# Four chained attention blocks on one core: splitting q and k straight out of the bank, VectorE masks on scores instead of probabilities, and a new step order

## The chip, the cores and the metric

One core of a Trainium2 chip runs the whole program in one launch. The metric is the device time of that core in microseconds (us), lower is better. Of the engines, PE (TensorE) multiplies and writes into eight accumulator banks of 128 partitions by 512 float32 ("bank"), ACT (ScalarE) and DVE (VectorE) read the banks and work in SBUF, POOL (GpSimd) works in SBUF alone here, and SP (SyncE) issues nearly all DMAs. Each engine runs its own instructions in order and waits for the others by semaphores.

## The reference

`x` is (32, 256, 256), `ctx_1024` is (32, 120, 256), all float32. Four blocks follow one another, and each batch element is independent of the others:

```
L0: x += causal self attention(LN(x));  x += cross attention(LN(x), ctx);  x += gelu-MLP(LN(x))
L1: x = LN(x + self attention(x), masked by mask_SxS_ik1); x = LN(x + cross attention(x, ctx)); x = LN(x + relu-MLP(x))
L2: x = LN(x + cross attention(x, ctx), masked by mask_BxSxS2_bk1)     16 heads of 16
L3: x = LN(x + cross attention(x, ctx))                                16 heads of 64
attention: scores = q.k / sqrt(d); masked ones -> minus infinity; p = softmax(scores); out = p.v
```

## The kernel before

**Passes.** Three passes of 32 elements each: l0, l1 and l2 (L2 and L3 together). Between passes x goes through DRAM. In each pass the elements are software-pipelined: several stages of neighbouring elements are in flight at once, and each engine's instruction stream interleaves them.

**What sets the order.** `LISTS` holds for each pass and engine one list of steps with due times, such as `scores_exp.own.0/1.3973`: kind, stage, index, and a time counted in elements. `Step` adds START of the pass and the element's number, `run` sorts all steps of an engine by that time, and this is the order in which the engine's code is written. The banks are handed out by a walk over PE's list: each PE step takes the bank that is free first, by the due time of the step that reads it. Due times only order; they never delay. `SPREAD` stretches the times of single elements at the ends of a pass. "own" is the first attention of a pass, "other" the second, "ff" the MLP, "three" is L3 and "c" the context.

**q and k in three bf16 parts.** For exact scores q and k are split as hi + mid + lo (bf16 each), and the parts are stacked along the contraction. Before the change: PE `project_q`/`project_k` fills a bank; ACT copies it with the bias into a float32 tile (`ot_raw`, for "other" inside `other_words`) and frees the bank; DVE casts hi (L949), subtracts it (L953) and casts mid (L959); POOL subtracts mid for lo (L663). SP spills each part to DRAM as it is ready (L519) and loads the stack back (L533, into `qstack`/`kstack`). PE `scores_max` then multiplies the stacks, DVE takes row maxima (L1002 with the mask added in the bank, L1006 without), splits them too (`negate`), PE turns them (`negate_t`), DVE copies them (`nm_t`, L1048), SP puts them below the stack as extra rows (`nm_rows`, L538), and PE's `scores_exp` makes transposed scores minus the maximum. ACT takes exp (L760) into `probs`, PE's `probs_v` multiplies by v.

**Masks at scores_exp.** l0 (causal): POOL zeroes the blocked half of the probabilities (L649). l1: for each of 16 heads PE adds the mask with one more matmul, `mask_less` by `identb`, 512 columns (`exp_on` = "pe"). l2: DVE takes the minimum of the probabilities and a mask after exp (`mask_probs`, L1022, `probs_own` and `m_cols`, both in SBUF).

**Normalisation** is DVE `stats` (L891 to L899), POOL `stats` (L594, L600), DVE `norm` (L911, `xh`), then a turn on PE (L1208) that ACT copies out.

## Time and profile before

| | us |
|---|---|
| median of 3 runs | 4791.93 |
| lowest, highest | 4788.07, 4794.76 |
| the profiled execution: its time, its span | 4792.18, 4790.4 |
| PE, PE's weight loads busy | 4512.8 (94%), 3551.8 (74%) |
| DVE, ACT, POOL busy | 3884.1 (81%), 2368.0 (49%), 1381.1 (29%) |

The page is one execution. Busy time of PE has modelled ends, so two matmuls that start 0.22 us apart can show 0.38 us each; the distance of starts tells the rate. The three passes have different limits, so the tables are read for stretches inside each: l0 until about 1510 us, l1 from about 1700 to 3090, l2 from about 3240. The half-speed slices of PE's clock stand at the start, at the borders of the passes, and singly in l2.

### The profile page before, as it was taken

To read this page: it belongs to the slowest core of one execution; us is meant where nothing else is said; L and a number is where in the kernel's file an instruction comes from. 1 tells how busy PE (TensorE), PEld (TensorE's weight loads), DVE (VectorE), ACT (ScalarE), POOL (GpSimd) and SP (SyncE) were. 2 spreads that over 40 slices of the span, in tenths; PEclk is the share of its full clock that TensorE was granted. 3 is DMA by queue.
4 is the path that set the end of the run, shared out by engine and by line. 5 is a ranking of instruction groups with operands and counts; after the bars stand their busy time and mean duration, and the time that the engine had idled before them with its cause. 6 is when DMAs were issued, how large, how long until landed. Compare 5 with 4: busy or idle time off the path is not lost. (4 is left out here: it accounts for less than half of the span.)

```text
span 4790.4 us, 97864 instructions
## 1 busy us (share of the span) xinstructions
PE 4512.8 (94%) x34560; PEld 3551.8 (74%) x34624; DVE 3884.1 (81%) x11141; ACT 2368.0 (49%) x6433; POOL 1381.1 (29%) x1813
## 2 busy tenths in 40 slices
PE   5999999999998899999999999979999999999998
PEld 4777777777777677777777777767777777777776
DVE  4888888888888788888888888857787787878786
ACT  2555555555454444444434343435555555555555
POOL 3333333333333133333323232321212121211212
PEclk8999999999999999999999999989999999999999
DMA  5444444444444444444444444321222212121221
GB/s 156 133 138 128 135 126 140 120 147 119 146 120 141 124 121 139 121 136 131 141 127 131 129 125 134 114 83 57 72 57 62 66 57 71 52 77 52 68 61 32
DMA packets 393272, 513.31 MB, mean 107 GB/s; under 512 B 109136, under 2 KB 360784, under 8 KB 371280
## 3 DMA queue, kind: packets, MB, share of 16 engines
q1 hardware_dynamic: 385392, 496.82, 35.5%
q10 hardware_dynamic: 7392, 10.24, 0.7%
q8 instruction: 276, 4.52, 0.4%
q14 instruction: 212, 1.74, 0.1%
HBM read 266.30 MB, written 236.72 MB: 105 GB/s over the span
## 5 line engine op out<-in xcount | busy, mean ns | idle before, releaser
L760 ACT ACTIVATE probs_own<-bank 128x384 f32<-128x384 f32 (+2 forms) x1280 | 598.2, 582 | 282.7 <-remote 156.5
L594 POOL TENSOR_SCALAR veps<-meanvar 128x2 f32<-128x2 f32 x256 | 63.1, 247 | 1503.3 <-DVE meanvar L899 1501.8
L1146 PE MATMUL bank<-ht,w_ff 128*128 128x256 f32 x2048 | 490.9, 383 | 0.8 <-issue 0.8
L1146 PE MATMUL bank<-w_ff,ffh 128*128 128x256 f32 x2048 | 491.1, 383 | 0.0
L1146 PE MATMUL bank<-qstack_own,kstack_own 99*128 99x256 bf16 (+2 forms) x2560 | 395.1, 265 | 31.9 <-DMA qstack_own<-nm_t_own 26.3
L1146 PEld LDWEIGHTS bank<-w_ff,ffh 128*128 128x128 f32 x2048 | 377.8, 192 | 46.8
L1146 PEld LDWEIGHTS bank<-ht,w_ff 128*128 128x128 f32 x2048 | 376.8, 191 | 46.9 <-issue 1.9
L1002 DVE CUSTOM_DVE_ANT_0 bank<-bank,mask_rows 128x256 f32<-128x256 f32 x1024 | 393.1, 474 | 2.9 <-PE bank L1146 2.9
L680 ACT ACTIVATE ht<-bank,columns_l 128x256 f32<-128x256 f32 x384 | 198.7, 578 | 382.8 <-PE bank L1208 382.6
L825 ACT ACTIVATE probs_other<-bank,negmax 128x120 f32<-128x120 f32 x1024 | 354.7, 382 | 64.4 <-DVE negmax L1126 64.2
L1146 PE MATMUL bank<-kstack_own,qstack_own 96*128 96x256 bf16 (+2 forms) x3072 | 355.4, 245 | 28.2 <-DMA qstack_own<-q_parts 19.9
L1146 PE MATMUL bank<-probs_own,v_aug_own 128*32 128x256 f32 (+2 forms) x5120 | 310.7, 368 | 53.7 <-DVE probs_own L1022 51.7
L1146 PEld LDWEIGHTS bank<-kstack_own,qstack_own 96*128 96x128 bf16 x3072 | 255.1, 98 | 107.7 <-issue 24.7
L1006 DVE TENSOR_REDUCE nmf_other<-bank 128x4 f32<-128x480 f32 x512 | 306.4, 644 | 33.8 <-PE bank L1146 33.4
L1146 PEld LDWEIGHTS bank<-qstack_own,kstack_own 99*128 99x128 bf16 (+1 forms) x2560 | 224.8, 105 | 142.9 <-DMA qstack_own<-nm_t_own 45.7
L1146 PE MATMUL bank<-ht,w_own 128*128 128x256 f32 x1280 | 314.4, 390 | 3.3 <-ACT ht L680 2.6
L760 ACT ACTIVATE probs_other<-bank 120x512 f32<-120x512 f32 x512 | 275.6, 607 | 76.0 <-PE bank L1146 75.9
L1002 DVE DVE_READ_ACCUMULATOR2_ANT nmf_own<- 128x1 f32 x2048 | 312.1, 152 | 0.0
L635 POOL TENSOR_TENSOR xb<-xh,vectors_l 128x512 f32<-128x512 f32 x160 | 213.5, 1334 | 289.6 <-issue 286.4
L663 POOL TENSOR_TENSOR other_parts<-other_words,other_parts 128x240 bf16<-128x240 f32 (+1 forms) x128 | 122.8, 970 | 580.1 <-issue 329.5
L1146 PEld LDWEIGHTS bank<-probs_own,v_aug_own 128*32 128x32 f32 (+1 forms) x5120 | 133.8, 109 | 187.8 <-DVE probs_own L1022 99.8
L1146 PEld LDWEIGHTS bank<-ht,w_own 128*128 128x128 f32 x1280 | 235.9, 192 | 46.5 <-issue 13.7
(166 smaller groups left out, 10673.6 us busy)
## 6 DMA issues: line engine op xcount, KB each, us to landing
qstack_own<-q_parts SPq DMA_DIRECT2D x96, 768.0 KB, 6.2
...
other_words<-k_parts SPq DMA_DIRECT2D x64, 360.0 KB, 3.7
```

The lines of the kernel that those rows point to most:

```text
L594: nc.gpsimd.tensor_scalar(veps[key][:, :], meanvar[key][:, :, 1], r["norms"][key]["eps"], None, ALU.add).then_inc(veps_ready.sem, 1)
L635: nc.gpsimd.tensor_tensor(xb[key][:, :, :], xh[src][:, :, :], mul[:, None, :].broadcast_to((P, QT, C)), ALU.mult).then_inc(xb_half.sem, 1)
L663: nc.gpsimd.tensor_tensor(f3[2], x32, f3[1], ALU.subtract).then_inc(lo_ready.sem, 1)
L680: return nc.scalar.activation(out, in_, ACT.Identity, scale=scale, bias=bias)
L760: nc.scalar.activation(probs[key][0:rows, j % a.slots, 0:n], bank_of(u)[0:rows, 0:n], ACT.Exp, scale=a.scale).then_inc(a_done.sem, 1)
L825: ins = nc.scalar.activation(probs3[:, j % 4, n, :], bank[:, n * S2:(n + 1) * S2], ACT.Exp, scale=-1.0, bias=negmax3[:, j, n:n + 1], accum ...
L1002: ins = v.tensor_tensor_reduce(scores, scores, add, -1.0, LIMIT if a.masked == "each" else 3.0e38, ALU.add, ALU.min, nmf[key][:, t, at:at ...
L1006: ins = v.tensor_reduce(nmf[key][:, t, first:first + FT * len(heads) - FT + 1:FT], bank[:, 0:len(heads) * nk].rearrange("p (h k) -> p h k" ...
L1146: return nc.tensor.matmul(out, lhsT, rhs, start=first, stop=True, skip_group_check=True)
```

## The change

1. **Split out of the bank.** ACT's copy to float32 goes. ACT writes hi (bf16) straight from the bank with the bias (`split_hi`). DVE computes (bank + bias) - hi into the float32 tile (`split_rest`; with a bias two SCALAR_TENSOR_TENSORs, one per half) and this frees the bank. ACT casts mid from that tile (`split_mid`). POOL's lo stays. Both DVE casts go.
2. **Masks of VectorE on scores.** `mask_probs` on DVE becomes `mask_scores`: DVE adds the mask (0 or -2^100) in the bank before exp, and exp waits for it. l2 does this for all 8 steps of an element. l1 goes from "pe" to "half": of 16 heads the 8 odd ones keep PE's mask matmul, the 8 even ones are masked by DVE. l0's POOL mask stays.
3. **l2's v copies.** `project_v` (now `project_v2`) and `project_v3` are copied out by ACT instead of DVE.
4. **New tables.** All of LISTS, START (l1 31.9 to 32.1, l2 64.4657 to 64.6), SPREAD emptied. Unused set-up of the old mask goes (`mask_cols`, a once-only PE step).

In the diff, `split_hi`, `split_mid` and the wait ahead of exp are ACT's code, the copy with `x32` as output and the addition of the mask are DVE's.

```diff
-START = {"l0": 0.0, "l1": 31.9, "l2": 64.4657}
+START = {"l0": 0.0, "l1": 32.1, "l2": 64.6}
-    "l0": {-2: (0.0, 0.9969)},
+    "l0": {},
...
-            turn.0.0/0.3084 project_q.own.0/0.6711 project_k.own.0/0.7099 scores_exp.own.0/1.4122 scores_exp.own.7/1.4222
+            turn.0.0/0.1721 split_hi_q.own.0/0.4346 split_hi_k.own.0/0.5024 split_mid_q.own.0/0.5224 split_mid_k.own.0/0.5687
...
+LAST_BY_DVE = {"project_q": "split_rest_q", "project_k": "split_rest_k"}
...
+            elif kind in ("split_hi_q", "split_hi_k"):
+                src = bank_of(u, ("project_" + x, key, 0))[:, 0:FT * nt].rearrange("p (f t) -> p f t", f=FT)
+                hi = parts[:, 0, :].rearrange("p (f t) -> p f t", f=FT)
...
+                if bias is None:
+                    copy(hi, src).then_inc(hi_ready.sem, 1)
+                else:
+                    nc.scalar.activation(hi[:, 0, :], src[:, 0, :], ACT.Identity, bias=bias[:, 0:1])
+                    nc.scalar.activation(hi[:, 1, :], src[:, 1, :], ACT.Identity, bias=bias[:, 1:2]).then_inc(hi_ready.sem, 1)
+            elif kind in ("split_mid_q", "split_mid_k"):
...
+                copy(parts[:, 1, :].rearrange("p (f t) -> p f t", f=FT), x32).then_inc(mid_ready.sem, 1)
...
+                if w.new(masked_by_dve, ("mask_scores", key, j)):
+                    act_e.wait_ge(masked_by_dve.sem, w.value(masked_by_dve, ("mask_scores", key, j)))
...
+                if bias is None:
+                    ins = v.tensor_tensor(x32, src, hi, ALU.subtract)
                 else:
+                    for f in range(FT):
+                        ins = v.scalar_tensor_tensor(x32[:, f, :], src[:, f, :], bias[:, f:f + 1], hi[:, f, :], ALU.add, ALU.subtract)
...
-                v.tensor_tensor(p, p, most, ALU.min).then_inc(masked_by_dve.sem, 1)
+                v.tensor_tensor(p, p, add, ALU.add).then_inc(masked_by_dve.sem, 1)
...
-              "dve", "pe")
+              "dve", "half")
```

What the tables move, at three places. First PE in l1, at the start of a burst of `scores_exp` of "own" (banks with their numbers; `d_done`, `a_done` are DVE's and ACT's counts). Before:

```order
L1146 MATMUL bank0<-qstack_own,kstack_own 128x256 [waits d_done]
L1146 MATMUL bank0<-qstack_own,kstack_own 128x256
L1146 MATMUL bank0<-mask_less,identb 128x512
L1146 MATMUL bank1<-qstack_own,kstack_own 128x256 [waits d_done]
L1146 MATMUL bank1<-qstack_own,kstack_own 128x256
L1146 MATMUL bank1<-mask_less,identb 128x512
L1146 MATMUL bank4<-qstack_own,kstack_own 128x256 [waits d_done]
L1146 MATMUL bank4<-qstack_own,kstack_own 128x256
L1146 MATMUL bank4<-mask_less,identb 128x512
```

After:

```order
L1156 MATMUL bank0<-qstack_own,kstack_own 128x256 [waits d_done]
L1156 MATMUL bank0<-qstack_own,kstack_own 128x256
L1156 MATMUL bank0<-mask_less,identb 128x512
L1156 MATMUL bank5<-qstack_own,kstack_own 128x256 [waits a_done]
L1156 MATMUL bank5<-qstack_own,kstack_own 128x256
L1156 MATMUL bank5<-mask_less,identb 128x512
...
L1156 MATMUL bank1<-qstack_own,kstack_own 128x256 [waits d_done]
L1156 MATMUL bank1<-qstack_own,kstack_own 128x256
L1156 MATMUL bank0<-qstack_own,kstack_own 128x256 [waits a_done]
L1156 MATMUL bank0<-qstack_own,kstack_own 128x256
L1156 MATMUL bank5<-qstack_own,kstack_own 128x256 [waits a_done]
L1156 MATMUL bank5<-qstack_own,kstack_own 128x256
```

Every head had its `mask_less` matmul; now only the odd ones have one, and the heads stand in an order that mixes both kinds, in more banks.

Second DVE in l1, around the splits of "own". Before (the splits of "own", `q_parts_own` and `k_parts_own`):

```order
L949 CAST q_parts_own<-ot_raw_own 128x512 [waits a_done,spilled_q_own]
L953 TENSOR_TENSOR ot_raw_own<-ot_raw_own,q_parts_own 128x512 [waits hi_ready]
L959 CAST q_parts_own<-ot_raw_own 128x512 [waits rest_ready,spilled_q_own]
L949 CAST k_parts_own<-ot_raw_own 128x512 [waits a_done,spilled_k_own]
L953 TENSOR_TENSOR ot_raw_own<-ot_raw_own,k_parts_own 128x512 [waits hi_ready]
L959 CAST k_parts_own<-ot_raw_own 128x512 [waits rest_ready,spilled_k_own]
L1107 TENSOR_TENSOR xn_own<-bank5,xb_0 128x512 [waits xhat_ready,xb_ready,d_full]
```

After (eight mask additions per element, `bank` and `mask_less`, stand among the other work; two stretches of it):

```order
L1032 TENSOR_TENSOR bank3<-bank3,mask_less 128x512 [waits a_full]
L1032 TENSOR_TENSOR bank1<-bank1,mask_less 128x512 [waits a_full]
L1032 TENSOR_TENSOR bank0<-bank0,mask_less 128x512 [waits a_full]
...
L1085 TENSOR_TENSOR ctx_q_own<-ot_raw_own,rec_own 128x2x8x16 [waits recip_ready]
L1085 TENSOR_TENSOR ctx_q_own<-ot_raw_own,rec_own 128x2x8x16
L984 SCALAR_TENSOR_TENSOR ot_raw_own<-bank1,columns_l1,q_parts_own 128x256 [waits divided,hi_ready]
L984 SCALAR_TENSOR_TENSOR ot_raw_own<-bank1,columns_l1,q_parts_own 128x256
L943 TENSOR_SCALAR xh_2<-xn_other,meanvar_2,rstd_2 128x256 [waits xb_half,rstd_ready,moments_ready]
L943 TENSOR_SCALAR xh_2<-xn_other,meanvar_2,rstd_2 128x256
L984 SCALAR_TENSOR_TENSOR ot_raw_own<-bank6,columns_l1,k_parts_own 128x256 [waits hi_ready]
L984 SCALAR_TENSOR_TENSOR ot_raw_own<-bank6,columns_l1,k_parts_own 128x256
```

Six instructions of the two splits have become four, each with a bank among its inputs, and `xh_2` stands between them.

Third POOL in l0, from the causal masks (L649) to the sums of the next stage. Before:

```order
L663 TENSOR_TENSOR k_parts_own<-ot_raw_own,k_parts_own 128x512 [waits spilled_k_own,mid_ready]
L594 TENSOR_SCALAR veps_1<-meanvar_1 128x2 [waits moments_ready]
L600 TENSOR_TENSOR rstd_1<-veps_1,half 128x2 [waits veps_ready,xhat_ready]
L663 TENSOR_TENSOR q_parts_own<-ot_raw_own,q_parts_own 128x512 [waits spilled_q_own,mid_ready]
L629 TENSOR_TENSOR xb_0<-x_in,vectors 128x512 [waits d_done,x_loaded]
L663 TENSOR_TENSOR other_parts<-other_words,other_parts 128x240 [waits spilled_k_other,mid_ready]
```

After:

```order
L664 TENSOR_TENSOR k_parts_own<-ot_raw_own,k_parts_own 128x512 [waits spilled_k_own,mid_ready]
L664 TENSOR_TENSOR q_parts_own<-ot_raw_own,q_parts_own 128x512 [waits spilled_q_own,mid_ready]
L634 TENSOR_TENSOR xb_0<-x_in,vectors 128x512 [waits d_done,x_loaded]
L599 TENSOR_SCALAR veps_1<-meanvar_1 128x2 [waits moments_ready]
L605 TENSOR_TENSOR rstd_1<-veps_1,half 128x2 [waits veps_ready,xhat_ready]
L634 TENSOR_TENSOR xb_1<-xn_own,vectors 128x512 [waits d_done]
```

`stats_1` (`veps_1`, `rstd_1`, which DVE's `xh_1` waits for) stood between the two lo parts, with `q_parts_own` and `xb_0` right behind it; now both lo parts and `xb_0` stand ahead of it.

## Rows read from the trace of the kernel before

**Rows 1.** The page, part 1: busy us (share of the span) x instructions.
```profile
PE 4512.8 (94%) x34560; PEld 3551.8 (74%) x34624; DVE 3884.1 (81%) x11141; ACT 2368.0 (49%) x6433; POOL 1381.1 (29%) x1813
```

**Rows 2.** Windows of 500 us in l0, l1, l2: length, busy of each engine, PEclk, DMA share, GB/s.
```profile
1000.00:1500.00 500.00, 470.75 (x3803) 382.72 (x3792) 424.13 (x910) 262.69 (x621) 180.36 (x299) 1.00 0.45 134
2000.00:2500.00 500.00, 498.35 (x3750) 390.23 (x3769) 435.18 (x1347) 218.57 (x475) 164.41 (x173) 1.00 0.46 136
...
3500.00:4000.00 500.00, 478.70 (x3592) 369.28 (x3591) 400.25 (x1343) 283.75 (x995) 100.03 (x104) 0.99 0.22 63
```

**Rows 3.** Tile nm_t_own on DVE, per pass: ns min/median/max, first and last start.
```profile
L1048 DVE COPY nm_t_own<-bank x30: 282/283/284, 136.1 to 1508.8; 48x256 bf16<-48x256 bf16 x30
...
L1048 DVE COPY nm_t_own<-bank x28: 273/274/282, 1732.1 to 3040.9; 48x256 bf16<-48x256 bf16 x28
...
L1048 DVE COPY nm_t_own<-bank x29: 281/283/284, 3339.8 to 4713.8; 48x256 bf16<-48x256 bf16 x29
```

**Rows 4.** Waits of PE, 1000 to 1500: us in total, times, longest.
```profile
PE bank L1208 <- DVE xh L911: 15.8, 11, 1.8
PE bank L1298 <- DVE nm_parts_own L1041: 7.5, 10, 0.9
PE bank L1146 <- DMA qstack_own<-nm_t_own: 5.7, 10, 0.7
```

**Rows 5.** Waits of PE, 2000 to 3000: the longest.
```profile
PE bank L1146 <- DMA qstack_other<-nm_t_other: 0.7, 3, 0.3
```

**Rows 6.** Waits of PE, 3500 to 4500: the longest.
```profile
PE bank L1146 <- DVE probs_own L1022: 33.4, 40, 1.1
```

**Rows 7.** Timeline of PE in l1: start us, us, instruction.
```profile
2414.68 0.38 PE L1146 MATMUL bank<-qstack_own,kstack_own 99*128 99x256 bf16 x2
2414.90 0.38 PE L1146 MATMUL bank<-mask_less,identb 128*128 128x512 bf16 x1
2415.12 0.38 PE L1146 MATMUL bank<-qstack_own,kstack_own 99*128 99x256 bf16 x2
```

**Rows 8.** Groups of DVE by form, 2000 to 3000: busy us, mean ns.
```profile
L953 DVE TENSOR_TENSOR ot_raw_own<-ot_raw_own,k_parts_own 128x512 f32<-128x512 f32 x20 | 30.5, 1526 | 0.7
...
L953 DVE TENSOR_TENSOR ot_raw_own<-ot_raw_own,q_parts_own 128x512 f32<-128x512 f32 x20 | 13.9, 693 | 0.7
...
L949 DVE CAST q_parts_own<-ot_raw_own 128x512 bf16<-128x512 f32 x20 | 8.5, 427 | 2.3
...
L959 DVE CAST other_parts<-other_words 128x240 bf16<-128x240 f32 x21 | 5.8, 278 | 0.0
```

**Rows 9.** Timeline of DVE in l1: reads of a bank, back to back.
```profile
2413.10 0.68 DVE L1107 TENSOR_TENSOR xn_ff<-bank,xb 128x512 f32<-128x512 f32 x1
2413.71 0.42 DVE L974 TENSOR_TENSOR other_words<-bank,vectors_l 120x256 f32<-120x256 f32 x1
2414.05 0.42 DVE L891 BATCH_NORM_STATS2 moments<-xn_ff 128x6 f32<-128x256 f32 x1
```

**Rows 10.** Timelines of DVE and POOL in l0, the same microseconds.
```profile
822.03 2.44 DVE L911 TENSOR_SCALAR xh<-xn_own,meanvar,rstd 128x256 f32<-128x256 f32 x2 [0.68 <-POOL rstd L600]
...
821.88 1.16 POOL L663 TENSOR_TENSOR q_parts_own<-ot_raw_own,q_parts_own 128x512 bf16<-128x512 f32 x1
823.00 1.31 POOL L629 TENSOR_TENSOR xb<-x_in,vectors 128x512 f32<-128x512 f32 x1
```

**Rows 11.** Lines L1022 and L1107 in l2, 3300 to 4700.
```profile
L1022 DVE TENSOR_TENSOR probs_own<-probs_own,m_cols x228: 677/680/1811, 3299.9 to 4675.6; 120x512 f32<-120x512 f32 x114
...
L1107 DVE TENSOR_TENSOR xn_own<-bank,x_in x29: 691/692/693, 3307.9 to 4681.8; 128x512 f32<-128x512 f32 x29
```

**Rows 12.** Timeline of DVE in l2: one element's masks.
```profile
3933.35 7.08 DVE L1022 TENSOR_TENSOR probs_own<-probs_own,m_cols 120x512 f32<-120x512 f32 x8 [0.72 <-ACT probs_own L760]
```

**Rows 13.** Groups of ACT, 500 to 1500: SBUF to SBUF.
```profile
L788 ACT ACTIVATE ff_xu<-ff_xu 128x512 f32<-128x512 f32 x84 | 53.5, 636 | 66.8 <-DVE ff_xu L1113 65.8 <-issue 1.0
```

**Rows 14.** Stack of k in l2: timeline of SP, median us to landing, timeline of PE.
```profile
3961.85 0.32 SPq L533 DMA_DIRECT2D kstack_own<-k_parts  x1
...
kstack_own<-k_parts SPq DMA_DIRECT2D x20, 360.0 KB, 6.0
...
3968.29 0.80 PE L1146 MATMUL bank<-kstack_own,qstack_own 96*128 96x120 bf16 x12
```

**Rows 15.** Timeline of PE at the border from l1 to l2.
```profile
3154.39 0.44 PE L1217 MATMUL bank<-identb,m_rows 128*120 128x128 bf16 x2 [10.02 <-DVE m_rows L925]
```

More of the change, by code:

```diff
@@ L46 @@
 PASSES = ("l0", "l1", "l2")
-START = {"l0": 0.0, "l1": 31.9, "l2": 64.4657}
+START = {"l0": 0.0, "l1": 32.1, "l2": 64.6}
+STAGE = {"own": 0, "0": 0, "x": 0, "c": 0, "m": 0, "other": 1, "1": 1, "ff": 2, "2": 2, "three": 2, "3": 2}
 SPREAD = {
-    "l0": {-2: (0.0, 0.9969)},
+    "l0": {},
     "l1": {},
@@ L120 @@
+            store.x.0/4.1837 loads.first.0/0.03 loads.rest.0/4.00 loads.rest.1/4.25 loads.rest.2/4.50 loads.rest.3/4.75
             loads.rest.4/5.00 loads.rest.5/5.25 loads.rest.6/5.50 loads.rest.7/5.75 loads.rest.8/6.00 loads.rest.9/6.25
@@ new lines @@
+            scores_max.own.0/1.4320 scores_max.own.1/1.4369 scores_max.own.5/1.4805 scores_max.own.4/1.4853
+            scores_max.own.7/1.4902 scores_max.own.3/1.5338 scores_max.own.6/1.5386 project_k3.three.0/1.5920
+            negate_t.own.0/1.6343 mask.m.0/1.6757 project_v2.own.0/1.6783 scores_exp.own.6/1.7102 scores_exp.own.4/1.7151
+            scores_exp.own.1/1.7201 scores_exp.own.3/1.7250 scores_exp.own.5/1.7397 scores_exp.own.7/1.7446
+            project_k3.three.1/1.7496 scores_exp.own.0/1.7897 scores_exp.own.2/1.7946 probs_v.own.2/1.8226 probs_v.own.3/1.8323
@@ L240 @@
+            nm_rows.own.0/1.6525 store.x.0/3.7906
         """,
@@ L357, in run @@
     when = {e: {(u.tag, u.element): u.at for u in steps} for e, steps in plan.items()}
-    masked = {(u.tag, u.element) for e in ("DVE", "POOL") for u in plan[e] if u.tag[0] == "mask_probs"}
+    masked = {(u.tag, u.element) for u in plan["POOL"] if u.tag[0] == "mask_probs"}
     banks = [ctx.enter_context(nc.psum_tensor(f"bank{i}", [P, 512], F32)) for i in range(8)]
@@ L366, in run @@
         _, b = min(free)
-        by = "ACT" if kind in READ_BY_ACT else "DVE"
-        read = (kind, key, j // 2) if kind == "probs_v" else u.tag
+        by = "ACT" if kind in READ_BY_ACT and kind not in LAST_BY_DVE else "DVE"
+        read = (kind, key, j // 2) if kind == "probs_v" else (LAST_BY_DVE[kind], key, 0) if kind in LAST_BY_DVE else u.tag
         holds[u.tag, u.element] = b, holder.get(b)
@@ L840, in _ @@
                      bank_of(u)[0:S2, :].rearrange("p (t f x) -> p t f x", t=QT, f=2)).then_inc(a_done.sem, 1)
+            elif kind == "project_v3":
+                if w.new(a_full, u.tag):
+                    act_e.wait_ge(a_full.sem, w.value(a_full, u.tag))
+                if first and j == r["first_of"]["project_v3"]:
+                    for x in "qk":
+                        reuse(act_e, w, u, spilled[x, "other"], [("spill_" + x, "other", i) for i in range(PARTS)], u.element - 1)
+                for tag in w.latest_first(a_full, [("probs_v3", "three", i) for i in range(2 * j, 2 * j + 2)], 1):
+                    if w.new(a_full, tag, 1):
+                        if w.twice:
+                            settle(act_e)
+                        act_e.wait_ge(a_full.sem, w.value(a_full, tag, 1))
+                copy(v3[:, 512 * j:512 * j + 512], bank_of(u)[0:S2, :]).then_inc(a_done.sem, 1)
             elif kind == "probs_v3":
@@ L1180, in _ @@
                 pe.wait_ge(setup_g, SETUP_ALL)
-            if kind == "masks":
-                pe.wait_ge(setup_v, len(make_masks[0]))
-                bank = take(u)
-                for t in range(QT):
-                    ins = nc.tensor.matmul(bank[:, t * P:(t + 1) * P], none_rows[:, t, :], ident[:, :], start=True, stop=True,
-                                           skip_group_check=True)
-                ins.then_inc(d_full.sem, 1)
-            elif kind == "context":
+            if kind == "context":
                 if w.new(c_loaded, ("load_c", "c", 0)):
```

480 lines of the change are left out of this document (222 added, 258 removed).

## The prediction

> **What bounds the kernel now.** I read the page first: PE is busy 94% of the span, DVE 81%, ACT 49% [rows 1]. An average over three passes says little, so next the windows, one inside each pass: PE is busy 470.75 of 500 us in l0, 498.35 in l1 and 478.70 in l2, DVE 424, 435 and 400 [rows 2]. l1 has no idle PE to give back, l0 and l2 have. The tile `nm_t_own` is written once per element, so its first and last start give the period of each pass [rows 3]: l0 (1508.8 - 136.1) / 29 = 47.33 us, l1 (3040.9 - 1732.1) / 27 = 48.47 us, l2 (4713.8 - 3339.8) / 28 = 49.07 us. Whatever the change does comes 31 times per pass through these three numbers; the rest is borders.
>
> Then PE's waits, divided by the elements in the window. In l0 500 / 47.33 = 10.6 elements: 15.8 us for `xh`, 7.5 us for `nm_parts_own` and 5.7 us for the DMA of the negated maxima [rows 4], which is 1.50, 0.71 and 0.54 us per element, 2.75 together. In l1 the longest wait is 0.7 us in 1000 [rows 5]: PE's own work is the limit. In l2 (1000 / 49.07 = 20.4 elements) the wait for DVE's masked probabilities is 33.4 us [rows 6], 1.64 us per element.
>
> **l1: eight mask matmuls less.** A `mask_less` matmul starts at 2414.90 and the next scores at 2415.12 [rows 7]: it takes 0.22 us of PE's pace (the 0.38 us shown is its modelled end). Eight go per element: 8 x 0.22 = 1.76 us. PE's floor becomes 48.47 - 1.76 = 46.7 us.
>
> DVE takes what PE gives, and it is the fuller of the others: 435.18 / 500 x 48.47 = 42.2 us per element [rows 2]. What changes there:
> - Added: eight additions over 512 columns of a bank. The trace has no plain addition that writes a bank, but a TENSOR_TENSOR reading a bank at 2413.10 lets the next one start at 2413.71 [rows 9], 0.61 us. Bounds for one: 0.6 us from that row, and above 1.53 us, the slowest row of a 512 column operation [rows 8]. I take 0.61, since operation, shape and source are the same: +4.9 us.
> - Removed: eight casts per element, six over 512 columns at up to 0.43 us and two over 240 at 0.28 [rows 8]: -3.1 us.
> - Changed: the subtraction, now out of the bank in two halves. Halves of 256 columns out of a bank are 0.34 us apart [rows 9], so 0.68 for two against 0.69 for the old one [rows 8], equal. But `k_parts_own`'s old subtraction took 1.53 us in the mean for the same work [rows 8]; if that goes, -0.8 us.
>
> Sum: +1.0 to +1.8 us, so DVE has 43.2 to 44.0 us of work in a period of at least 46.7. It still fits, with 2.7 to 3.5 us to spare instead of 6.3. With less room some handoffs will show on PE; l0 and l2 show 2.75 and 2.0 us of idle PE at more room than that, though from single slow operations. I charge 0.5 us (bounds 0 and 1.76, where nothing is left of the gain): l1 gains 1.25 us per element.
>
> **l2: the mask ahead of exp.** Masks of one element take 7.08 us for eight [rows 12], and PE's `probs_v` waits for them. The operation's median is 0.68 us and its maximum 1.81 [rows 11]: it is the same work each time, stretched by something. An addition of the same size with one operand in a bank shows 691 to 693 ns over 29 elements [rows 11], never stretched. In l0 the trace shows such a stretch beside POOL's work [rows 10], so I put this one down to POOL too. The Trainium skill, page "SBUF — State Buffer", section "Who interferes with whom", says that DVE and GpSimd share a pair of SBUF ports as an exclusive lock, and the section before it that a DVE operation takes the lock with two SBUF inputs or in a two-port mode; the trace agrees (1811 against 693 ns). By that rule the mask in the bank costs 8 x 0.61 = 4.9 us; without it, if POOL slowed this one too, still 7.08. I take the row that never stretches. The chain from the first mask to the last is then 2.2 us shorter, more than the 1.64 us that PE waits. What is late next is exp, which now runs behind the mask: one 0.6 us ACT operation after the last mask instead of one mask after the last exp, so the end comes no later. I count 1.3 of the 1.64 us. ACT takes three more bank copies per element (0.6 us each or less) at 283.75 / 500 busy [rows 2]: hidden by ACT's idle time, and it is behind nothing that PE waits for except in its own queue. Bounds 0 and 1.64.
>
> **l0: nothing leaves PE, two stalls may.** PE's 1.50 us are for `xh` of "own": its two halves take 2.44 us at 822.03 while POOL runs lo of q from 821.88 and the sum `xb` from 823.00 [rows 10]. In the new POOL order both stand ahead of `stats_1`, so at `xh_1` POOL has nothing queued but the next stage's sum. That stall should go, and `nm_parts_own`'s 0.71 likewise, if POOL's `xb` no longer meets it. The DMA's 0.54 stays. That would be 2.2 us; but `stats_1` now stands behind lo of q, which hangs on ACT and DVE, and a stall removed lets the next one through. I take 1.5 us, bounds 0 and 2.75. The dropped casts and the moved `split_mid` change no length on PE; DVE loses 3.1 us here and gains nothing, which is only room.
>
> **The split's chain.** Before: ACT copy, DVE hi, DVE rest, DVE mid, POOL lo. After: ACT hi, DVE rest, ACT mid, POOL lo. One DVE step of 0.43 us [rows 8] is gone from the chain, mid costs ACT about 0.64 us (an SBUF to SBUF operation of 512 columns [rows 13]) instead of 0.43, so it is 0.2 us shorter, plus one more crossing between engines. The hi part is ready one step earlier. ACT's work: four mids of 0.64 us or less, four hi in place of four copies. It matters, since the lead is small: in l2 SP issues the load of k's stack at 3961.85, it lands 6.0 us later at 3967.85, and PE uses it at 3968.29 [rows 14]. Every cast mid waits in ACT's queue behind exps. I count 0 (bounds -0.2 and +2 us per element). The bank of a projection is held longer, until `split_rest`; the new order has room for it, as it mixes banks more. SP issues the same loads and spills in a slightly other order.
>
> A page speaks against splitting out of the bank. The Trainium skill, page "VectorE: DVE Perf Modes", section on the TRN2 errata, gives a higher fixed cost for a PSUM source than for an SBUF one (120 against 58 cycles) and per instruction, so two halves would cost 0.78 us against 0.59 for one whole. By it DVE has 0.7 us per element more in l1 and still fits. The trace does not show this price: halves from a bank are 0.34 us apart [rows 9].
>
> **Borders.** At 3154.39 PE waits 10.02 us for the mask rows of the first element of l2 [rows 15]; the new PE list has that `mask` step half an element later, so it should go. Against it stands that all splits of a border have new neighbours, and the first stages of l1 start 0.2 elements later by START. I count 0, bounds -15 and +15 us.
>
> **Sum.** 31 x (1.5 + 1.25 + 1.3) = 31 x 4.05 = 126 us. Profiled span 4790.4, with 1.8 us around it 4792.2, which is the median of the runs (4791.93). 4792 - 126 = 4666 us.
>
> **Rivals.**
> 1. *DVE becomes the bound of l1.* For: slack falls from 6.3 to about 3 us, mask additions sit between PE and exp, and exp runs in its own order, so one late mask holds all exps behind it. Against: 43 to 44 us of work in 46.7. Then l1 gains nothing, and l0 and l2 get what is above: 31 x 2.8 = 87, or with half of that lost too 60: 4705 to 4732, say 4720.
> 2. *The stalls of l0 and l2 only move.* For: both are ends of long chains, where another link may be next. Against: both are traced to one stretched operation. Then only l1's gain stays: 31 x 1.25 = 39, at most 55: 4745.
> 3. *All idle PE goes.* l0 2.75, l1 1.76, l2 2.0: 31 x 6.5 = 202: 4590. For: less contention in every pass. Against: the DMA wait of l0 is untouched.
> 4. *Slower: mid is stuck in ACT's queue.* Place: `split_mid` of q or k, behind a row of 8 or more exps of 0.5 us, then lo, spill and stack load late, with PE's `scores_max` waiting. The lead of 0.44 us in l2 [rows 14] covers nothing. It outweighs the gain when the stack is over 126 / 93 = 1.4 us late per element. At 3 us late in all passes: 93 x 3 - 126 = +153: 4945; in one pass alone, 31 x 3 more and its own gain lost, 4790 to 4800.
> 5. *The reordering undoes it.* A step order by due times that does not fit the real durations gives new waits of about 1.3 us per element: no change, 4790.
>
> **How the numbers follow.** The forecast 0.55 (own range 4625 to 4705), rival 1 0.16, rival 2 0.12, rival 3 0.05, rival 4 0.08, rival 5 0.04. A measurement of this kernel tells about 0.2% (10 us) from no change. The range 4610 to 4755 holds the forecast, rivals 1 and 2 and half of 3. Faster 0.88, within 0.2% 0.04, slower 0.08.
>
> **What would show it.** Period of `nm_t_own`: 45.8 in l0, 47.2 in l1, 47.8 in l2. In l1 half as many `mask_less` matmuls on PE, PE still over 97% busy, DVE near 44 us of each element. In l2 the mask additions on banks at 0.68 us each with no long maximum, and `probs_v` no longer waiting for DVE for over 0.3 us. In l0 `xh_1` at 0.4 us per half. Wrong would be: mask additions over 0.8 us, PE waits in l1 over 1 us per element that end with DVE or ACT, or `scores_max` waiting for stack DMAs.

## The result, and the profile after

The changed kernel takes 4522.95 us (median of 4 runs, 4519.09 to 4525.0), the kernel before 4791.87: a ratio of 0.9438, 95% interval 0.9422 to 0.9455. That is 269 us less, where I had forecast 126 and a range that ended at 4610. The page, part 1, answers to [rows 1]:

```profile
PE 4377.2 (97%) x34368; PEld 3536.8 (78%) x34368; DVE 3512.6 (78%) x10917; ACT 2551.7 (56%) x6849; POOL 1376.6 (30%) x1813
```

The tile `nm_t_own`, one stretch inside each pass, as in [rows 3]:

```profile
L1058 DVE COPY nm_t_own<-bank x29: 275/283/283, 173.4 to 1399.1; 48x256 bf16<-48x256 bf16 x29
...
L1058 DVE COPY nm_t_own<-bank x26: 270/273/274, 1664.0 to 2838.7; 48x256 bf16<-48x256 bf16 x26
...
L1058 DVE COPY nm_t_own<-bank x30: 270/273/274, 3126.2 to 4442.9; 48x256 bf16<-48x256 bf16 x30
```

First to last start over the count less one gives the periods:

| us per element | before | forecast | after | change |
|---|---|---|---|---|
| l0 | 47.33 | 45.8 | 43.78 | -3.55 |
| l1 | 48.47 | 47.2 | 46.99 | -1.48 |
| l2 | 49.07 | 47.8 | 45.40 | -3.67 |

31 x (3.55 + 1.48 + 3.67) = 270: the periods carry the whole gain, and the borders, taken together, add nothing to it. l1 came out near the forecast. The surprise is l0 and l2.

PE's waits in l0, 500 to 1400 in both kernels, each in us, times, longest. Before, which answers to [rows 4] over more elements:

```profile
PE bank L1208 <- DVE xh L911: 27.0, 19, 1.8
PE bank L1298 <- DVE nm_parts_own L1041: 13.8, 19, 0.7
PE bank L1146 <- DMA qstack_own<-nm_t_own: 10.9, 19, 0.7
```

After, the only one:

```profile
PE bank L1156 <- DMA qstack_own<-nm_t_own: 0.2, 1, 0.2
```

All three stalls are gone, the DMA's among them. In l2 nothing waits for a masked probability any more ([rows 6] had 33.4 us).

But idle PE before was only 2.75 and 2.0 us per element. Windows inside l0 and l2 (length, PE, PEld, DVE, ACT, POOL busy, PEclk, DMA share, GB/s) show the rest. Before:

```profile
500.00:1350.00 850.00, 800.33 (x6510) 650.02 (x6509) 720.29 (x1546) 447.19 (x1059) 310.74 (x522) 1.00 0.44 131
3500.00:4400.00 900.00, 861.60 (x6470) 666.21 (x6469) 717.84 (x2410) 510.48 (x1773) 176.94 (x186) 0.99 0.22 63
```

After:

```profile
500.00:1350.00 850.00, 849.67 (x7023) 707.75 (x7022) 699.72 (x1595) 518.82 (x1229) 344.38 (x561) 1.00 0.49 144
3500.00:4400.00 900.00, 898.85 (x6992) 725.00 (x6992) 659.16 (x2488) 589.04 (x2003) 184.82 (x196) 1.00 0.23 68
```

Busy share times period: in l0 PE was busy 800.33 / 850 x 47.33 = 44.56 us per element and is now busy 43.76, for the same 362 matmuls (6510 / 850 x 47.33 and 7023 / 850 x 43.78). In l2 it was 46.98 and is 45.34. So 0.8 and 1.6 us of "busy" time did no work. A matmul is drawn 0.38 us long while the next starts 0.22 us later [rows 7]; when the next one is late, that drawn end covers the first 0.16 us of the wait. In l2 half-clock stretches add to it (PEclk 0.99). By my estimate this accounts for 3 waits x 0.16 = 0.5 of the 0.8 us in l0, and for 4 x 0.16 + 0.01 x 49 = 1.1 of the 1.6 us in l2; where the rest lies I did not find.

The other half of the story is on DVE. Groups by form (count, busy us, mean ns), l0 (500 to 1450) and l2 (3340 to 4710) before:

```profile
L911 DVE TENSOR_SCALAR xh<-xn_own,meanvar,rstd 128x256 f32<-128x256 f32 x40 | 48.7, 1257 | 14.0 <-POOL rstd L600 14.0
L1041 DVE TENSOR_TENSOR nm_parts_own<-nmf_own,nm_parts_own 128x32 bf16<-128x32 f32 x20 | 22.8, 1138 | 0.7
...
L1022 DVE TENSOR_TENSOR probs_own<-probs_own,m_cols 120x512 f32<-120x512 f32 x224 | 198.0, 952 | 20.6 <-ACT probs_own L760 20.6
L953 DVE TENSOR_TENSOR ot_raw_own<-ot_raw_own,k_parts_own 128x240 f32<-128x240 f32 x28 | 38.0, 1358 | 0.0
```

After (500 to 1390, 3130 to 4440):

```profile
L943 DVE TENSOR_SCALAR xh<-xn_own,meanvar,rstd 128x256 f32<-128x256 f32 x42 | 15.5, 411 | 30.1 <-POOL rstd L605 30.1
L1051 DVE TENSOR_TENSOR nm_parts_own<-nmf_own,nm_parts_own 128x32 bf16<-128x32 f32 x20 | 3.8, 192 | 0.7
...
L1032 DVE TENSOR_TENSOR bank<-bank,m_cols 120x512 f32<-120x512 f32 x232 | 141.7, 692 | 2.4 <-PE bank L1156 1.0
L981 DVE TENSOR_TENSOR ot_raw_own<-bank,k_parts_own 128x240 f32<-128x240 f32 x29 | 11.8, 408 | 24.4 <-ACT k_parts_own L678 24.4
```

These four were stretched before (1257, 1138, 952, 1358 ns). The first two are the same instructions and now run at their plain length (411, 192); the other two read a bank in place of SBUF and are never stretched (692, 408). One operation of l0 has taken the stretch over, where it holds up nobody: `ffh` takes 854 ns, where it took 662 in the kernel before.

```profile
L1129 DVE SCALAR_TENSOR_TENSOR ffh<-ff_xu 128x512 f32<-128x512 f32 x83 | 70.8, 854 | 0.0
```

### The profile page after: what moved, and what is told of

Read it like the earlier page. It is cut to its first block and busy times, and to the rows that moved or that the text cites. A ratio compares the mean times of both kernels' runs of the same rounds, so it can differ in the third digit from the quotient of the medians.

```text
span 4520.2 us, 97208 instructions
## 1 busy us (share of the span) xinstructions
PE 4377.2 (97%) x34368; PEld 3536.8 (78%) x34368; DVE 3512.6 (78%) x10917; ACT 2551.7 (56%) x6849; POOL 1376.6 (30%) x1813
## 5 line engine op out<-in xcount | busy, mean ns | idle before, releaser
L1156 PEld LDWEIGHTS bank<-w_ff,ffh 128*128 128x128 f32 x2048 | 379.8, 190 | 47.7 <-ACT ffh L793 0.2
L1156 PEld LDWEIGHTS bank<-ht,w_ff 128*128 128x128 f32 x2048 | 373.8, 191 | 45.7 <-issue 0.8
L1156 PE MATMUL bank<-qstack_own,kstack_own 99*128 99x256 bf16 (+2 forms) x2560 | 365.5, 263 | 16.5 <-DMA qstack_own<-nm_t_own 15.3
L640 POOL TENSOR_TENSOR xb<-xh,vectors_l 128x512 f32<-128x512 f32 x160 | 203.5, 1272 | 386.9 <-DVE xn_other L1117 311.1
L1156 PE MATMUL bank<-probs_own,v_aug_own 128*32 128x256 f32 (+2 forms) x5120 | 286.1, 362 | 8.8 <-ACT probs_own L783 5.2
L1136 DVE TENSOR_REDUCE negmax<-bank 128x4 f32<-128x480 f32 x256 | 158.2, 649 | 159.4 <-PE bank L1156 159.4
L1013 DVE CUSTOM_DVE_ANT_0 bank<-bank,m_rows 128x120 f32<-128x120 f32 x1024 | 248.7, 326 | 20.7 <-PE bank L1156 20.7
```

Of the source, the lines that this page charges most:

```text
L640: nc.gpsimd.tensor_tensor(xb[key][:, :, :], xh[src][:, :, :], mul[:, None, :].broadcast_to((P, QT, C)), ALU.mult).then_inc(xb_half.sem, 1)
L1013: ins = v.tensor_tensor_reduce(scores, scores, add, -1.0, LIMIT if a.masked == "each" else 3.0e38, ALU.add, ALU.min, nmf[key][:, t, at:at ...
L1136: v.tensor_reduce(negmax3[:, j, :], bank_of(u)[:, 0:HG * S2].rearrange("p (h k) -> p h k", k=S2), AX_X, ALU.min).then_inc(negmax3_ready.se ...
L1156: return nc.tensor.matmul(out, lhsT, rhs, start=first, stop=True, skip_group_check=True)
```

## The experiments

Fifteen kernels, each timed against the kernel before on the same chip; that one's median was between 4788.6 and 4792.1 us each time. Differences to the kernel after are between times of different rounds. The periods are means over elements 3 to 28 of l0, and over as many steady ones of l1 and l2, from the starts of `nm_t_own`.

| kernel | us | ratio to before (95%) | l0 | l1 | l2 |
|---|---|---|---|---|---|
| before | 4791 | 1 | 47.3 | 48.5 | 49.1 |
| after | 4523 | 0.9438 (0.9422 to 0.9455) | 43.8 | 47.0 | 45.4 |
| order_alone | 4937 | 1.0305 (1.029 to 1.032) | 47.1 | 51.3 | 51.4 |
| code_alone | 4868 | 1.0161 (1.0146 to 1.0176) | 47.3 | 53.3 | 47.1 |
| narrow_before | 4612 | 0.9624 (0.9608 to 0.964) | 44.9 | 48.2 | 46.4 |
| narrow_after | 4513 | 0.9419 (0.9405 to 0.9433) | 43.7 | 47.0 | 45.4 |
| order_narrow | 4717 | 0.9841 (0.9826 to 0.9856) | 44.7 | 50.5 | 47.4 |
| code_narrow | 4760 | 0.9924 (0.9904 to 0.9944) | 44.8 | 52.8 | 47.1 |
| pool_order_before | 4841 | 1.0103 (1.0086 to 1.012) | 48.9 | 48.5 | 49.0 |
| mask_bank_before | 4751 | 0.9917 (0.9902 to 0.9932) | 47.3 | 48.5 | 47.7 |
| pool_order_after | 4555 | 0.951 (0.9496 to 0.9524) | 44.8 | 47.0 | 45.3 |
| mid_on_vector | 4576 | 0.9551 (0.9535 to 0.9567) | 45.2 | 47.3 | 45.4 |
| l1_masks_pe | 4572 | 0.9544 (0.9530 to 0.9558) | 43.8 | 48.8 | 45.4 |
| project_v_early | 4579 | 0.9555 (0.9539 to 0.9571) | 45.7 | 47.0 | 45.4 |
| l1_twelve_masks | 4599 | 0.9599 (0.9584 to 0.9613) | 43.8 | 49.5 | 45.4 |
| mask_sbuf_after | 4702 | 0.9807 (0.9793 to 0.9822) | 43.8 | 47.0 | 51.3 |
| l1_tuned | 4530 | 0.9453 (0.9437 to 0.9469) | 43.7 | 47.2 | 45.4 |

### The two halves apart

In the cuts from the tables, here and below, entries of one engine stand side by side and the ones between them are left out; in the cuts of code `...` marks what is left out.

order_alone: the old code under the new tables (k of own in l0 shown):

```diff
-START = {"l0": 0.0, "l1": 31.9, "l2": 64.4657}
+START = {"l0": 0.0, "l1": 32.1, "l2": 64.6}
-ACT project_k.own.0/0.5390   DVE split_hi_k 0.5779, split_rest_k 0.5883, split_mid_k 0.6046
+ACT project_k.own.0/0.5315   DVE split_hi_k 0.5535, split_rest_k 0.5537, split_mid_k 0.5738
```

> The old code with the new tables of times: PE, ACT, POOL and SyncE in the new order; ACT still copies q and k out of the bank, DVE casts hi and mid and masks the probabilities of l2 in SBUF, PE makes all sixteen masks of l1. Two copies of l1 stand a little later than the new hi parts, since they must follow the division of the heads. Theory A (the order takes the stalls of l0 and l2 away, whatever the code): periods l0 44.2, l1 48.3, l2 46.8 us, in all 4792 - 31 x (3.1 + 0.2 + 2.3) = 4618. Theory B (the moved work does it: less on DVE, the mask in the bank, the split out of the bank; the order only adapts): the old code under the new order keeps or worsens its stalls, 4760 to 4830. Theory C (POOL no longer runs beside DVE's SBUF operations): as A in l0, where the order of POOL is the new one (44.2), but l2 keeps stretched masks and stays near 48: 4670.

Measured 4937: slower than before by 146 us, worse than any theory had. Its DVE groups in l0:

```profile
L957 DVE TENSOR_TENSOR ot_raw_own<-ot_raw_own,q_parts_own 128x512 f32<-128x512 f32 x20 | 29.7, 1486 | 0.7
L963 DVE CAST other_parts<-other_words 128x240 bf16<-128x240 f32 x20 | 27.0, 1348 | 0.0
L915 DVE TENSOR_SCALAR xh<-xn_own,meanvar,rstd 128x256 f32<-128x256 f32 x40 | 14.7, 410 | 27.7 <-POOL rstd L604 27.7
```

The new order does free `xh`. But POOL now works beside the subtraction for q and the cast of mid, and those take 1486 and 1348 ns. They are the very operations that the new code reads out of the bank or gives to ACT. l0 as a whole gains nothing (47.1). In l1, which loses 2.8 us, PE waits 21.8 us in 1000 for `ctx_t_own` and the subtraction for k is still at 1530 ns; with POOL's work cut (order_narrow, below) they are 5.1 us and 693 ns. In l2 PE waits over 3 us at a time for the masked probabilities, and then something more is lost. Timeline of PE, then windows around the wait:

```profile
3523.33 1.16 PE L1150 MATMUL bank<-vectors,probs_other 64*128 64x120 f32 x16
3527.73 3.45 PE L1150 MATMUL bank<-probs_own,v_aug_own 120*32 120x256 f32 x32 [3.24 <-DVE probs_own L1026]
3531.11 3.77 PE L1150 MATMUL bank<-w_v,ct 128*120 128x512 f32 x4
...
3538.16 1.88 PE L1150 MATMUL bank<-w_v,ct 128*120 128x512 f32 x4
```

```profile
3515.00:3527.00 12.00, 9.31 (x77) 8.11 (x75) 9.06 (x18) 6.28 (x12) 6.96 (x6) 1.00 0.08 25
3528.00:3536.00 8.00, 7.86 (x52) 2.94 (x44) 5.27 (x11) 1.48 (x8) 0.00 (x0) 0.57 0.00 0
3536.00:3550.00 14.00, 14.00 (x87) 10.76 (x84) 9.85 (x24) 10.70 (x37) 3.40 (x4) 1.00 0.29 85
```

After 3.24 us without a matmul the granted clock over 3528 to 3536 is 0.57, so most of this stretch is at the lower of its two levels (1.2 GHz), and the four matmuls of `w_v` take 3.77 us where the next four take 1.88. Over l2 the grant is 0.96 (3500 to 4400).

code_alone: the new code under the old tables; each step stands where the one that it replaces stood:

```diff
-DVE split_hi_k.own.0/0.5779 split_rest_k.own.0/0.5883 split_mid_k.own.0/0.6046
+ACT split_hi_k.own.0/0.5390 split_mid_k.own.0/0.6046   DVE split_rest_k.own.0/0.5883
```

> The new code with the old tables of times: each new step stands where the step it replaces stood (hi on ACT at the old copy, rest and mid at their old times, the masks just ahead of their exp). Theory A: the stalls of l0 stay (46.5 to 47.3), l1 gains at most its eight matmuls (47.3), l2 loses the wait for the masks alone (47.5): 4792 - 31 x (0.4 + 1.2 + 1.5) = 4696. Theory B: most of the gain is here, below 4620. Theory C: in l2 the mask in the bank no longer stretches (692 ns each instead of 952), l2 47.5; in l0 the stretched xh stays, because POOL's order is the old one: 4700.

Measured 4868. In l0 nothing moves (47.3): `xh` still takes 1255 ns beside POOL. In l2 the mask in the bank takes 2.0 us off, somewhat more than expected. In l1 the additions stand in the chain from PE to exp, and PE waits for exp; the window of l1 has the granted clock at 0.95 too, by my estimate 0.05 x 53.3 = 2.7 us per element beside the 3 us of waits:

```profile
PE bank L1161 <- ACT probs_own L788: 57.2, 73, 2.3
```

```profile
2000.00:3000.00 1000.00, 938.81 (x6725) 699.68 (x6723) 804.20 (x2498) 448.64 (x949) 297.41 (x323) 0.95 0.40 119
```

So each half alone loses (+146 and +76), and together they gain 269. None of the three theories had said that.

### Contention taken away

narrow_before, narrow_after, order_narrow, code_narrow: the same edit to the kernels before and after, order_alone and code_alone. It leaves out all but 32 columns of POOL's residual sums and lo subtractions, so these four don't compute the full result.

```diff
+            few = C if u.element % NB == 0 else 32
...
-nc.gpsimd.tensor_tensor(xb[key][:, :, :], x[:, :, :], add[:, None, :]...
+nc.gpsimd.tensor_tensor(xb[key][:, :, 0:few], x[:, :, 0:few], add[:, None, 0:few]...
...
-nc.gpsimd.tensor_tensor(f3[2], x32, f3[1], ALU.subtract)...
+nc.gpsimd.tensor_tensor(f3[2][:, :, 0:few], x32[:, :, 0:few], f3[1][:, :, 0:few], ALU.subtract)...
```

> The kernel before, but GpSimd's residual sums and lo subtractions cover 32 of the 256 (120) columns in all elements but the first of a pass: that part of the computation is left out. Same order, same instructions, GpSimd's big SBUF operations shortened to about a fifth. Theory C: xh of l0 falls from 1257 to 410 ns, the masks of l2 from 952 to 690, periods l0 45, l1 48.2, l2 46.8, in all 4792 - 31 x (2.3 + 0.3 + 2.3) = 4640. Theory A with no part for contention: the operations keep their length and the time stays above 4760.

> The kernel after, with the same part of GpSimd's work left out. All theories: PE has under 0.1 us idle per element in l0 and l2, so there is little left to gain: 4500 to 4523. More than 30 us of gain would say that contention still costs time which the idle rows don't show.

> The old code in the new order (4937 us) with GpSimd's residual sums and lo subtractions cut to 32 columns in all elements but the first of a pass; that part of the computation is left out. Contention theory: its stalls come from casts and subtractions stretched beside GpSimd (CAST of other_parts 811 ns, the subtraction for q 1485), so l0 falls from 47.1 to 44.3, l2 from 51.3 to 48.5 where the stretched masks go but still stand behind exp, l1 from 51.3 to 50: 4937 - 31 x 6.9 = 4723. Theory that the order does not fit the old code's chains: under 60 us of gain, above 4875.

> The new code in the old order (4868 us) with the same part of GpSimd's work left out. Contention theory: l0's xh (1255 ns) and nm_parts (1143 ns) shrink, l0 from 47.2 to 44.7; l1's wait of 3 us for exp is a chain and stays (53.3 to 52.7), l2 from 47.1 to 46.3: 4868 - 31 x 3.9 = 4747. Theory of chains alone: l0 stays above 46.5, time above 4830.

Two groups of narrow_before in l0, and its only wait of PE there:

```profile
L916 DVE TENSOR_SCALAR xh<-xn_own,meanvar,rstd 128x256 f32<-128x256 f32 x40 | 14.8, 412 | 14.0 <-POOL rstd L604 14.0
L1046 DVE TENSOR_TENSOR nm_parts_own<-nmf_own,nm_parts_own 128x32 bf16<-128x32 f32 x19 | 3.7, 197 | 0.7
```

```profile
PE bank L1151 <- DMA qstack_own<-nm_t_own: 11.7, 20, 0.7
```

In the same order, with the same instructions, `xh` and `nm_parts_own` are at their plain length and both stalls are gone; the DMA's stays, as it should. The edit is worth 179 us to the kernel before (expected 151), 220 to order_alone (expected 214), 108 to code_alone (expected 121) and 10 to the kernel after (expected up to 23). It also shortens lo itself by some 0.85 us (1158 to 302 ns for q), so these numbers are upper ends for contention alone.

Read as a sum: with POOL's work cut, the change is worth 4612 - 4513 = 99 us. The other 170 of its 269 us come with POOL's work, and contention is at most that much, since the shorter lo is in it.

Contention doesn't explain why either half alone loses. With POOL's work cut, the new order alone still costs 4717 - 4612 = 105 us and the new code alone 4760 - 4612 = 148. Together the halves are better than their sum by 146 + 76 + 269 = 491 us with POOL's full work and by 105 + 148 + 99 = 352 with it cut. So most of what they do for each other is not contention; I read it as the steps of this code fitting this order, and no run takes that apart.

### Single parts, put in or taken back

pool_order_before, in the kernel before:

```diff
-POOL split_lo_k.own.0/0.6201 stats.1.0/1.6659 split_lo_q.own.0/0.6910 xb.0.0/0.7162
+POOL xb.0.0/0.6 split_lo_k.own.0/0.6201 split_lo_q.own.0/0.65 stats.1.0/1.6659
```

> The kernel before with two entries of GpSimd's table of l0 moved: its residual sum of x and its lo of q stand ahead of the statistics of the next element, not behind them. Nothing else moves. The theory of contention: VectorE's xh, which starts as GpSimd's rstd is ready, then meets an idle GpSimd and takes 410 ns a half instead of 1257, PE's 1.5 us for it go, and with what hides under modelled ends up to 1.8: l0 45.6, time 4792 - 31 x 1.7 = 4739. The theory that the stall only moves: the statistics come up to 1.4 us later, xh starts later by as much, l0 stays above 46.8, time above 4775.

A miss: slower by 49 us. `xh` is down to 411 ns as expected, but PE waits for it 46.7 us in 900 instead of 27.0. The timeline of POOL says why:

```profile
847.90 1.28 POOL L632 TENSOR_TENSOR xb<-x_in,vectors 128x512 f32<-128x512 f32 x1 [9.09 <-DVE xn_own L1110]
849.13 1.61 POOL L666 TENSOR_TENSOR k_parts_own<-ot_raw_own,k_parts_own 128x512 bf16<-128x512 f32 x1
850.71 1.60 POOL L666 TENSOR_TENSOR q_parts_own<-ot_raw_own,q_parts_own 128x512 bf16<-128x512 f32 x1
852.28 0.21 POOL L597 TENSOR_SCALAR veps<-meanvar 128x2 f32<-128x2 f32 x1
```

The sum needs the buffer that DVE's `xn_own` empties, so it holds both lo behind it, and the statistics, which PE's chain needs, stand behind all three. A stretched operation was exchanged for a queue. Half-clock stretches come on top: the grant is 0.99 in l0.

pool_order_after, the reverse in the kernel after:

```diff
-POOL split_lo_q.own.0/0.6437 xb.0.0/0.6706 stats.1.0/1.6991   SP spill_q.own.2/0.6757
+POOL stats.1.0/1.6991 split_lo_q.own.0/0.71 xb.0.0/0.72       SP spill_q.own.2/0.715
```

> The kernel after with the reverse: in GpSimd's table of l0 the lo of q and the residual sum of x stand behind the statistics of the next element again, as before. The theory of contention: xh of own stretches back to about 1250 ns a half, PE waits about 1.5 to 1.8 us for it: l0 45.4, time 4523 + 31 x 1.6 = 4573. The theory that the new order has slack for it: under 4535.

`xh` is stretched again and nothing else is:

```profile
L948 DVE TENSOR_SCALAR xh<-xn_own,meanvar,rstd 128x256 f32<-128x256 f32 x40 | 48.9, 1263 | 28.0 <-POOL rstd L610 28.0
```

```profile
PE bank L1221 <- DVE xh L948: 16.7, 20, 1.1
```

Mechanism as expected, size smaller: l0 +1.0 us per element, +32 us in all (expected 50).

mid_on_vector, the kernel after with the casts of mid back on DVE:

```diff
-mid_ready = counts("mid_ready", "ACT", ("split_mid_q", "split_mid_k"))
+mid_ready = counts("mid_ready", "DVE", ("split_mid_q", "split_mid_k"))
...
```

> The kernel after with mid of all splits cast by VectorE again, at the times that ACT had for them; hi by ACT and rest out of the bank stay. If the new code pays because VectorE has fewer SBUF operations that meet GpSimd, then these casts stretch in l0 (811 ns instead of 277 as the order alone showed) and some of the stalls come back: l0 44.5, l1 47.5, l2 45.6, time 4523 + 31 x 1.4 = 4566. If the place of the cast is indifferent (VectorE has 7 us free per element): 4523 to 4530.

```profile
L970 DVE CAST other_parts<-other_words 128x240 bf16<-128x240 f32 x20 | 27.0, 1350 | 0.0
```

```profile
PE bank L1311 <- DVE nm_parts_own L1055: 21.8, 20, 1.1
```

4576, +53 us, close to the expected +43. In l0 one cast of 0.28 us now takes 1350 ns, and PE waits for `nm_parts_own`, which DVE makes later (21.8 us, after none).

project_v_early, the kernel after with one step of l0 moved back on PE (and on DVE):

```diff
-PE negate_t.own.0/1.1518 project_v.own.0/1.1545 scores_exp.own.2/1.2297
+PE project_v.own.0/0.6355 ... negate_t.own.0/1.1518 scores_exp.own.2/1.2297
```

> The kernel after with project_v of own in l0 ahead of the maxima again, where it stood before, instead of between negate_t and the scores for exp. If that step is what covers the DMA of the negated maxima, PE's wait for the DMA returns: 0.54 us on the page per element before, 0.7 with what lies under modelled ends: l0 44.5, time 4523 + 31 x 0.7 = 4545. If the DMA is covered anyway: 4520 to 4526.

```profile
PE bank L1161 <- DMA qstack_own<-nm_t_own: 20.3, 19, 1.5
PE bank L1161 <- DMA qstack_other<-q_parts: 5.1, 8, 1.6
```

4579, +56 us: l0 +1.9 us, more than the expected 0.7, since the stack of other is now late as well. The eight matmuls of project_v between negate_t and the scores are what covers the DMA.

l1_masks_pe, the kernel after with PE adding all masks of l1:

```diff
-              "dve", "half")
+              "dve", "pe")
```

> The kernel after with all sixteen masks of l1 added by PE again; VectorE's eight are gone. By the pace of 0.22 us a mask matmul l1 goes from 46.99 to 48.75: 4523 + 31 x 1.76 = 4578. If the waits of l1 (for the stack of the negated maxima and for nm_parts, about 0.5 us per element) came from VectorE's additions, they go, and the time is 4523 + 31 x 1.3 = 4563.

4572; l1 goes from 46.99 to 48.76, 1.77 us, against 8 x 0.22 = 1.76. PE's small waits of l1 (2000 to 2800) stay, so the additions did not cause them. In the kernel after, then here:

```profile
PE bank L1156 <- DMA qstack_own<-nm_t_own: 5.9, 17, 0.5
...
PE bank L1159 <- DMA qstack_own<-nm_t_own: 5.9, 17, 0.5
```

l1_twelve_masks, one step further:

```diff
-        return self.exp_on == "pe" or self.exp_on == "half" and j % 2 == 1
+        return self.exp_on == "pe" or self.exp_on == "half" and j in (5, 7, 11, 13)
...
```

> The kernel after with twelve of the sixteen masks of l1 added by VectorE instead of eight, each placed just ahead of its exp; four stay with PE. PE has 4 x 0.22 = 0.9 us less: 4523 - 28 = 4495, if nothing waits. VectorE has 40.1 + 4 x 0.69 = 42.9 us in 46.1. If the chain from scores over the mask to exp becomes the limit, as in the new code under the old order (3 us per element for exp), l1 gets slower: up to 4523 + 31 x 1 = 4554. I take 4505.

A miss: 4599, 76 us slower than after.

```profile
PE bank L1162 <- ACT probs_own L789: 23.4, 40, 1.0
PE bank L1313 <- ACT probs_own L789: 22.3, 20, 1.1
```

DVE has time left (42.6 busy of 49.5 us), yet PE waits for exps that wait for masks in DVE's queue. Of none, eight and twelve masks on DVE, the three that ran in this order, eight is the fastest.

mask_bank_before, the kernel before with the mask of l2 alone moved into the bank (`p` is `probs_own`, behind exp, in the first line and the bank, ahead of exp, in the second), and mask_sbuf_after, the reverse in the kernel after:

```diff
-v.tensor_tensor(p, p, most, ALU.min)...
...
+v.tensor_tensor(p, p, add, ALU.add)...
```

> The kernel before with one part of the change: in l2 VectorE adds the mask to the scores in the bank ahead of exp, instead of the minimum on the probabilities in SBUF behind it; the order is the old one with each mask just ahead of its exp. The theory of contention: the operation takes 692 ns and not 952, PE's wait of 1.64 us for it goes, with 0.4 to 0.8 more that lay under modelled ends; l2 47.0, time 4792 - 31 x 2.0 = 4730. The theory that order is what counts: PE now waits for exp instead, 48.5, time 4775.

> The kernel after with l2's mask again as a minimum on the probabilities in SBUF behind exp, in the new order. GpSimd has only 10 us of work per element in l2. If stretching was most of the mask's cost, the place beside GpSimd decides: 952 to 1028 ns again and PE waiting about 3.2 us per element for probabilities as in the old code under this order: l2 48.9, 4523 + 31 x 3.5 = 4632. If the new order keeps the masks clear of GpSimd: 4535 to 4560.

Under the old order it is worth 1.36 us per element of l2 (4751; expected 2.0), since part of the wait moves to exp. Under the new order taking it back costs 5.9 us (4702; expected 3.5):

```profile
PE bank L1170 <- DVE probs_own L1034: 54.3, 20, 3.4
```

```profile
3500.00:4400.00 900.00, 843.36 (x6199) 651.39 (x6200) 623.61 (x2163) 528.25 (x1794) 178.26 (x174) 0.95 0.21 61
```

3.1 us of it are the wait (54.3 us in 900 / 51.3 = 17.5 elements), the rest is about what a clock of 0.95 costs (0.05 x 51.3 = 2.6). The mask's stretch in the kernel before has its partner in the trace, as my prediction had supposed without showing it. POOL there, during the 7.08 us of [rows 12]:

```profile
3933.41 1.77 POOL L635 TENSOR_TENSOR xb<-xh,vectors_l 128x512 f32<-128x512 f32 x1
3935.26 1.61 POOL L639 TENSOR_TENSOR xb<-xb,vectors_l 128x512 f32<-128x512 f32 x1
3944.63 1.27 POOL L635 TENSOR_TENSOR xb<-xh,vectors_l 128x512 f32<-128x512 f32 x1 [7.76 <-issue]
```

Both sides pay: the same POOL operation takes 1.77 us beside the masks and 1.27 us without them.

l1_tuned, an attempt to beat the kernel after, three entries of PE's table of l1 (and DVE's negate_t with the first):

```diff
-PE negate_t.own.0/1.1405 scores_max.other.4/2.2731 scores_max.other.0/2.3419
+PE negate_t.own.0/1.1505 scores_max.other.4/2.209 scores_max.other.0/2.21
```

> The kernel after with three entries of PE's table of l1 moved: negate_t of own one step later, two maxima of other (0.43 us of PE's work) ahead of the first scores for exp instead of between them. They cover PE's two remaining waits of l1, 0.18 us for nm_parts and 0.35 us for the DMA of the negated maxima: 4523 - 31 x 0.4 = 4511. If negate_t's later start delays the DMA by as much as is covered: 4520 to 4530.

4530 (4524 to 4533), so no gain: the intervals of the two ratios overlap. The DMA wait goes (7.3 to 1.2 us in 1000), but l1's period is 47.2, not shorter than 47.0; where it went I did not find. None of the kernels that compute everything is faster than the kernel after.

## Why the prediction was wrong

The direction was right, and so were the stalls and the price of a mask matmul that the gain was built on. Two terms of the sum were too small, and behind one of them two mechanisms were wrong: what covers the DMA, and what the dropped casts are worth.

- *l1, 1.25 us.* Measured 1.48. The price of the mask matmul held exactly (l1_masks_pe). DVE's load did not: I had 43.2 to 44.0 us of work per element, it is 40.1, because more stretched operations shrank than the one I had counted: `xh` (848 and 886 ns, now 412 and 407) and the casts of `nm_parts_other` (643 and 940 ns, now 172 and 182). I had taken `k_parts_own`'s 1526 ns as the only one that might go. The price of an addition held: 0.60 us from start to start, against 0.61. My 0.5 us was for DVE's lack of room, yet what is left of waits is there without the additions too (l1_masks_pe). So it is in part luck that the term came near.
- *l0, 1.5 us: this step failed.* Measured 3.55. I counted 2.75 us of idle and took half of it, arguing that "the DMA's 0.54 stays" and that a stall removed lets the next one through. The DMA wait went because project_v now stands in it; I had the new PE order before me and did not look at what lies between negate_t and the scores. The two others went together because they had one cause, POOL beside DVE (narrow_before removes both and adds no new one). And 0.8 us more lay in PE's busy time, where the idle rows show nothing.
- *"The dropped casts ... which is only room."* Wrong: mid_on_vector costs 53 us. The casts did not matter by their 3.1 us but as partners that POOL's operations would meet in the new order.
- *l2, 1.3 us: this step failed too.* Measured 3.67. For the mask alone under the old order the figure was right (1.36, mask_bank_before). But I let the pass gain nothing else. `k_parts_own`'s subtraction (1358 ns) shrank, the half-clock stretches went (PEclk 0.99 to 1.00), and 1.6 us in all had been counted as busy.
- *Split chain 0, borders 0.* Both held in sum. Inside the passes PE does not wait for the stacks' parts. At the border from l1 to l2 the 10.02 us wait went, as forecast, but others of 7.7 us (`nm_parts_other`) and 6.5 us (the stack of q) stand there now: the zero is a balance and not an absence.
- *Rival 3, "all idle PE goes", 4590,* was the nearest. I gave it 0.05, against the DMA wait; and its price was bounded by idle time, which is no upper bound for what stalls cost. The lower end of my range rested on the same bound.
- *Rival 5, the reordering undoes it,* describes order_alone (+146 us). That it did not come about is due to the code change: with it the same order gives the fastest kernel.

What held of the Trainium skill's rule in "SBUF — State Buffer", section "Who interferes with whom" (an exclusive lock between DVE and GpSimd): the runs agree. A DVE operation of 32 columns goes from 192 to 1138 ns, about the length of one POOL operation (1.16 us), while the mask additions on a bank have means of 687 to 692 ns and no one over 700 in every kernel that has them. I had used that rule for the masks of l2 and had not applied it to the whole list of SBUF operations. The higher fixed cost of "VectorE: DVE Perf Modes", section on the TRN2 errata, did not decide anything, but the estimate of 0.78 us for two halves that I had worked out from it came closer than my 0.68 from the trace. In the kernel after the two halves of a split start 0.36 to 0.40 us apart (448 to 480 ns drawn). My 0.34 us was a misreading: the operation that starts 0.34 us after the half in [rows 9] is the statistics' and reads SBUF. Nothing hung on it, with DVE at 699.72 / 850 x 43.78 = 36.0 us of work in l0's 43.78. Plain additions of half a bank do start 0.33 us apart (`v_aug_own`, l1 before), so the bank alone does not make the difference.

What stays open: with POOL's work cut, l1 takes 50.5 us under the new order alone and 52.8 under the new code alone. The sizes can be placed. In order_narrow PE is idle 35.4 us in 1000, 1.8 us per element, above the 48.76 that sixteen mask matmuls take in l1_masks_pe. In code_narrow it waits 46.5 us in 1000 for exp and has a grant of 0.94; 56.1 us of idle are 3.0 per element, and the clock costs 0.06 x 52.8 = 3.2 by my estimate, above the 47.0 of the kernel after. Which step of the orders holds up the chains no run has singled out. And the 170 us for contention include the shorter lo.
